# Delta sublayer: where a unit's corner and joining product stand among the next unit's doublings

## The reference, cut to what matters

```python
q, k, v = (silu(causal_conv4(x @ W)) for W in (Wq, Wk, Wv))      # conv over tokens, 4 taps
alpha, beta = sigmoid(x @ Wa + ba), sigmoid(x @ Wb + bb)
def step(S, (qt, kt, vt, at, bt)):                                # one token after another
    err = S @ kt - vt
    S = at * S - bt * err * kt.T
    return S, S @ qt
o = layernorm(scan(step)(q, k * DK**-0.5, v, alpha, beta))
out = (o * sigmoid(x @ Wg)) @ Wo
```

## Time and profile before

| what | value |
|---|---|
| median of 3 runs | 3333.66 us (3332.99 to 3333.68) |
| profiled execution, its own time | 3329.28 us |
| span in that execution | 3327.5 us |
| PE busy | 3193.5 us (96%) |
| PEld busy | 2639.1 us (79%) |
| DVE busy | 2411.1 us (72%) |
| ACT busy | 1955.1 us (59%) |
| POOL busy | 827.1 us (25%) |
| doubling products with d_power, L1652 | 4096 records, 142.2 us |
| taps on DVE, L1404 | 1116 records, 624.0 us |

### The profile page before, as it was taken

The page is one execution under the profiler, slowest core; times in us unless marked ns, Lnnn a source line. Parts: engine busy times, 40 slices in busy tenths (PEclk is TensorE's granted clock), DMA queues, the critical chain, the costliest instruction groups (busy, mean ns, idle before and its releaser), DMA issues. The chain is left out here.

```text
span 3327.5 us, 89349 instructions
## 1 busy us (share of the span) xinstructions
PE 3193.5 (96%) x34218; PEld 2639.1 (79%) x34218; DVE 2411.1 (72%) x7923; ACT 1955.1 (59%) x4769; POOL 827.1 (25%) x828
## 2 busy tenths in 40 slices
PE   6999989999999999999999969999799999999999
PEld 5888878888888888888888858788667777777787
DVE  4777778777778878787878637777666777777764
ACT  3565556666666666666666626565465555555553
POOL 2333322232222223232322223333200111111100
PEclk9999999999999999999999979999999999999999
DMA  6000000000000000000000040000000000000000
GB/s 242 1 1 1 1 8 27 22 21 18 15 18 25 18 25 18 22 16 21 21 22 21 9 163 1 1 1 1 1 1 1 1 1 1 1 5 5 5 8 10
DMA packets 51337, 66.84 MB, mean 20 GB/s; under 512 B 4962, under 2 KB 40290, under 8 KB 49378
## 3 DMA queue, kind: packets, MB, share of 16 engines
q1 hardware_dynamic: 50914, 61.13, 5.8%
HBM read 58.56 MB, written 2.56 MB: 18 GB/s over the span
## 5 line engine op out<-in xcount | busy, mean ns | idle before, releaser
L1404 DVE SCALAR_TENSOR_TENSOR d_acc<-d_raw,d_taps,d_acc 128x255 f32<-128x255 f32 x1116 | 624.0, 600 | 128.0 <-ACT d_raw L1392 114.8
L2485 ACT ACTIVATE s_probs<-s_probs,s_nmax 128x128 f32<-128x128 f32 (+1 forms) x768 | 286.8, 446 | 176.7 <-DVE s_nmax L203 176.0
L1659 ACT COPY d_power<-bank 128x768 f32<-128x768 f32 x320 | 259.5, 811 | 134.7 <-PE bank L1652 134.7
L203 DVE CUSTOM_DVE_ANT_0 s_probs<-bank,mask 128x128 f32<-128x128 f32 (+1 forms) x768 | 225.5, 349 | 105.7 <-PE bank L2466 105.6
L746 POOL TENSOR_TENSOR a_q<-a_rope 64x512 f32<-64x512 f32 x128 | 165.0, 1289 | 534.4 <-DVE a_recip L814 313.6
L1390 ACT ACTIVATE d_acc<-bank,d_tap_bias,d_taps 128x256 f32<-128x256 f32 x372 | 190.4, 563 | 148.0 <-PE bank L1368 138.2
L783 ACT ACTIVATE a_area<-a_area,a_nmax 128x128 f32<-128x128 f32 (+1 forms) x512 | 226.4, 443 | 85.6 <-DVE a_nmax L203 84.9
L203 DVE CUSTOM_DVE_ANT_0 a_area<-bank,mask 128x128 f32<-128x128 f32 (+1 forms) x512 | 159.0, 355 | 133.3 <-PE bank L764 130.9
L809 ACT COPY a_area<-bank 128x512 f32<-128x512 f32 (+1 forms) x260 | 137.3, 580 | 117.8 <-PE bank L800 117.8
L736 DVE TENSOR_TENSOR a_rope<-bank,a_sinT 32x512 f32<-32x512 f32 x256 | 177.4, 693 | 5.7
L1807 POOL TENSOR_TENSOR d_o_rs<-d_o_var,minus_half 128x4 f32<-128x4 f32 x64 | 69.6, 1088 | 419.7 <-DVE d_o_var L1801 419.7
(11 more groups left out here) (287 smaller groups left out, 8702.0 us busy)
## 6 DMA issues: line engine op xcount, KB each, us to landing
d_alpha<-d_alpha_rows SPq DMA_DIRECT2D x64, 256.0 KB, 3.6
d_g_decay<-d_running_rows SPq DMA_DIRECT2D x32, 258.0 KB, 3.5
a_w_o<-in_a_w_o SPq DMA_DIRECT2D x2, 2048.0 KB, 16.6
a_area<-in_a_q_nope SPq DMA_DIRECT2D x2, 1536.0 KB, 8.1
x<-in_x SPq DMA_DIRECT2D x8, 256.0 KB, 16.0
d_wk<-in_d_wk SPq DMA_DIRECT2D x1, 2048.0 KB
d_wq<-in_d_wq SPq DMA_DIRECT2D x1, 2048.0 KB
d_wv<-in_d_wv SPq DMA_DIRECT2D x1, 2048.0 KB
```

The costliest lines, as they stand in the source:

```text
L203: return core.nc.vector.tensor_tensor_reduce(out=out, in0=scores, in1=core.mask[:, blocks], scale=-1.0, scalar=HIGHEST, op0=ALU.add, op1=A ...
L1404: last = nc.vector.scalar_tensor_tensor(out=convolved(G, r)[:, j, d:T], in0=raw[:, r % 2, j, 0:T - d], scalar=taps[:, r // 2, h, 3 - d:4 - ...
L1659: nc.scalar.copy(power[:], b_step[:, :, 0:3 * P]).then_inc(g.step_out, 1)
L2485: last = nc.scalar.activation(own, own, ACT.Exp, scale=-1.0, bias=nmax[:, s % 2, t, i:i + 1])
```

## The change

Corner and join of unit e = u - 1 move from the end of round u - 1 into round u: corner ahead of doubling 0, join ahead of doubling 1 (behind kk and ab), and y from behind doubling 0 to behind doubling 1. A round then has six blocks of small tiles. Corner's product now goes to b_join (the banks of y and o) and no longer to the last columns of b_step, so the waits for those banks move from join to corner. Both get semaphores of their own (close_in_psum, close_out), and a unit has six steps on the old ones. ACT's queue gets the same order: corner's copy, doubling 0's copy, [ab], join's copy, doubling 1's copy, y's copy, then the sigmoids. Nothing is computed otherwise, and no DMA is moved.

```diff
--- before.py
+++ after.py
@@ -1150,7 +1150,7 @@
 UNITS = NB * CHUNKS
 ALL_GROUPS = NB * GROUPS
 LEVELS = 6
-STEPS = LEVELS + 2
+STEPS = LEVELS
 HALF = P // 2
 TAPS = 4
 RPG = 8
@@ -1181,6 +1181,7 @@
         self.k_in_psum, self.k_ready = sem("d_k_in_psum"), sem("d_k_ready")
         self.kq_decayed = sem("kq_decayed")
         self.step_in_psum, self.step_out = sem("d_step_in_psum"), sem("d_step_out")
+        self.close_in_psum, self.close_out = sem("d_close_in_psum"), sem("d_close_out")
         self.y_in_psum, self.y_ready = sem("dy_in_psum"), sem("dy_ready")
         self.yw_ready = sem("yw_ready")
         self.state_in_psum, self.state_ready = sem("state_in_psum"), sem("state_ready")
@@ -1495,7 +1496,7 @@
 
         def n_act(act, u):
             act.wait_ge(g.n_in_psum, u + 1)
-            need(act, g.step_in_psum, STEPS * (u - 2) + LEVELS + 1)
+            need(act, g.close_in_psum, 2 * (u - 2) + 1)
             nc.scalar.copy(wide(n0[u % 2][:]), b_kk[:, :]).then_inc(g.n_ready, 1)
 
         def k_pe(pe, u):
@@ -1599,7 +1600,7 @@
 
             if l == 0:
                 pe.wait_ge(g.n_ready, u + 1)
-            need(pe, g.step_out, STEPS * u + l if l > 0 else STEPS * u - 1)
+            need(pe, g.step_out, STEPS * u + l)
             lo_a = 2 * P
 
             def tile(s, r, lo, width):
@@ -1669,45 +1670,45 @@
         def corner_pe(pe, u):
 
             pe.wait_ge(g.step_out, STEPS * u + LEVELS)
-            for j in range(GH):
-                pair, c = j // 2, j % 2
-                cols = slice(3 * P + pair * HALF, 3 * P + (pair + 1) * HALF)
-                nc.tensor.matmul(b_step[half(c), 0, cols], tT[half(0), u % 2, j, half(0)],
-                                 core.ident[half(0), half(0)], start=True, stop=True,
-                                 tile_position=(0, c * HALF), skip_group_check=True)
-                last = nc.tensor.matmul(b_step[half(c), 1, cols], n0[u % 2][half(1), j, half(0)],
-                                        tT[half(1), u % 2, j, half(1)], start=True, stop=True,
-                                        tile_position=(HALF, c * HALF), skip_group_check=True)
-            last.then_inc(g.step_in_psum, 1)
-
-        def corner_act(act, u):
-            act.wait_ge(g.step_in_psum, STEPS * u + LEVELS + 1)
-            nc.scalar.copy(corner[:], b_step[:, :, 3 * P:4 * P]).then_inc(g.step_out, 1)
-
-        def join_pe(pe, u):
-
-            pe.wait_ge(g.step_out, STEPS * u + LEVELS + 1)
             need(pe, g.y_ready, u)
             need(pe, g.oT_affine, u)
             need(pe, g.rhs_ready, (u + 1) // 2 if u % 2 == 1 else 0)
             for j in range(GH):
                 pair, c = j // 2, j % 2
                 cols = half(pair)
+                nc.tensor.matmul(b_join[half(c), 0, cols], tT[half(0), u % 2, j, half(0)],
+                                 core.ident[half(0), half(0)], start=True, stop=True,
+                                 tile_position=(0, c * HALF), skip_group_check=True)
+                last = nc.tensor.matmul(b_join[half(c), 1, cols], n0[u % 2][half(1), j, half(0)],
+                                        tT[half(1), u % 2, j, half(1)], start=True, stop=True,
+                                        tile_position=(HALF, c * HALF), skip_group_check=True)
+            last.then_inc(g.close_in_psum, 1)
+
+        def corner_act(act, u):
+            act.wait_ge(g.close_in_psum, 2 * u + 1)
+            nc.scalar.copy(corner[:], b_join[:, :, 0:P]).then_inc(g.close_out, 1)
+
+        def join_pe(pe, u):
+
+            pe.wait_ge(g.close_out, 2 * u + 1)
+            for j in range(GH):
+                pair, c = j // 2, j % 2
+                cols = half(pair)
                 last = nc.tensor.matmul(b_join[half(0), c, cols], corner[half(c), 0, cols],
                                         corner[half(c), 1, cols], start=True, stop=True,
                                         tile_position=(c * HALF, 0), skip_group_check=True)
-            last.then_inc(g.step_in_psum, 1)
+            last.then_inc(g.close_in_psum, 1)
 
         def join_act(act, u):
-            act.wait_ge(g.step_in_psum, STEPS * (u + 1))
+            act.wait_ge(g.close_in_psum, 2 * (u + 1))
             heads = tT[half(0), u % 2, :, half(1)].rearrange("p (q s) t -> p s q t", s=2)
             nc.scalar.copy(heads, b_join[half(0), :, 0:P].rearrange("p s (q t) -> p s q t", q=2))\
-                .then_inc(g.step_out, 1)
+                .then_inc(g.close_out, 1)
 
 
         def y_pe(pe, e):
             c = e % 2
-            pe.wait_ge(g.step_out, STEPS * (e + 1))
+            pe.wait_ge(g.close_out, 2 * (e + 1))
             if c == 0:
                 pe.wait_ge(g.v_ready, e + 1)
             else:
@@ -1871,16 +1872,20 @@
                 for u in range(UNITS + 1):
                     e, n, q = u - 1, u % CHUNKS, rounds_of(u)
                     live = u < UNITS
+                    if e >= 0:
+                        corner_pe(pe, e)
                     if live:
                         step_pe(pe, u, 0)
-                    if e >= 0:
-                        y_pe(pe, e)
                     if u + 1 < UNITS:
                         kk_pe(pe, u + 1)
                     if n == CHUNKS - 2 and u + 2 < UNITS:
                         ab_pe(pe, u // CHUNKS + 1)
+                    if e >= 0:
+                        join_pe(pe, e)
                     if live:
                         step_pe(pe, u, 1)
+                    if e >= 0:
+                        y_pe(pe, e)
                     if q is not None:
                         project_pe(pe, q)
                     if live:
@@ -1910,15 +1915,12 @@
                         oT_pe(pe, e)
                     if live:
                         qk_pe(pe, u)
-                        corner_pe(pe, u)
                     if q is not None:
                         project_pe(pe, q + 3)
                     if e >= 0:
                         out_pe(pe, e)
                     if n == CHUNKS - 3 and u + 3 < UNITS:
                         xnT_pe(pe, u // CHUNKS + 1, q + 4)
-                    if live:
-                        join_pe(pe, u)
 
             @block.vector
             def _(dve):
@@ -1972,18 +1974,22 @@
                     e, n, G, q = u - 1, u % CHUNKS, u // 2, rounds_of(u)
                     live, odd = u < UNITS, u % 2
                     ahead = G + 1 if G + 1 < ALL_GROUPS and live else None
+                    if e >= 0:
+                        corner_act(act, e)
                     if live:
                         step_act(act, u, 0)
+                    if n == CHUNKS - 2 and u + 2 < UNITS:
+                        ab_act(act, u // CHUNKS + 1)
+                    if e >= 0:
+                        join_act(act, e)
+                    if live:
+                        step_act(act, u, 1)
                     if e >= 0:
                         y_act(act, e)
                     if odd and ahead is not None:
                         sigmoid_act(act, ahead, 2)
                     if not odd and u < UNITS:
                         sigmoid_act(act, G, 5)
-                    if n == CHUNKS - 2 and u + 2 < UNITS:
-                        ab_act(act, u // CHUNKS + 1)
-                    if live:
-                        step_act(act, u, 1)
                     if q is not None:
                         evacuate_act(act, q)
                     if live:
@@ -2009,16 +2015,12 @@
                         oT_act(act, e)
                     if ahead is not None:
                         sigmoid_act(act, ahead, 4 if odd else 1)
-                    if live:
-                        corner_act(act, u)
-                        if not odd:
-                            k_act(act, u)
+                    if live and not odd:
+                        k_act(act, u)
                     if q is not None:
                         evacuate_act(act, q + 3)
                     if n == CHUNKS - 3 and u + 3 < UNITS:
                         xnT_act(act, u // CHUNKS + 1, q + 4)
-                    if live:
-                        join_act(act, u)
 
             @block.gpsimd
             def _(pool):
```

## The result

The changed kernel takes 3354.29 us, the median of 4 runs (3348.10 to 3357.00), against 3333.67 (3332.99 to 3334.84) for the kernel before: a ratio of 1.0059, 95% interval 1.0041 to 1.0076. It is 20.6 us slower; 17.9 were forecast, in a range of 3338 to 3360. The profiled execution took 3357.00, with a span of 3355.2. One execution of the kernel before, in the comparison of e8, took 8075.17 us, a slow one; ratios and spreads here go by the fast runs alone.

What follows compares the result with a forecast made beforehand. TensorE's order was taken as the bound, with waits on POOL and DVE. Odd rounds to state 20.6, out - 9.6, even beginnings + 7.5, round 0 - 0.6: + 17.9 us, median 3351.6, range 3338 to 3360.

Steps and rivals of the forecast that it cites:

- out's restart of 0.10: On TensorE, a block following a wait costs 0.10 us more; charged to out, leaving an odd round 0.31 gained.
- Part 1: Corner's own block goes, 0.57 us less TensorE work per round; out's wait for POOL leaves 0.31 odd, 0 even.
- Rival A: The block on TensorE is saved in every round with no wait in its place: 20.4 us less, 3313; chance 0.06.
- Part 2: Corner merged with doubling 0 stays at 1.24 us; join ahead of doubling 1 adds 0.25 to every round's beginning.
- Part 3: y behind doubling 1, kk directly behind doubling 0: order sums to 0, but kk newly waits 0.56 to 0.89 in odd rounds.
- Rival B: kk finds its d_kT in time because DVE's even-round work slides forward: + 1.2 us, 3335, no change; chance 0.11.
- Rival C: Chain corner, copy, join, copy, y runs late behind doubling 1, adding 6 to 12 us: 3358 to 3364; chance 0.08.
- the 0.57 of round 37: Round 37's odd-round delay before state: kk's new wait for d_kT on TensorE, entered in its sum as 0.57 us.
- the 0.53: State's existing wait for DVE's d_yw in round 37, 0.53 us, which was to go as kk's new wait swallows it.

Runs made afterwards that it cites:

- e8: The kernel before with one edit, d_yw ahead of the third taps on DVE in odd rounds: 3326.24 us against 3333.36, ratio 0.9980.
- e3: The kernel before without its corner products and their copy, join reading a tile of zeros: 3322.88 us against 3333.76, ratio 0.9968.
- e5: The changed kernel with every join product done twice, same operands and place: 3368.26 us, 14.0 more than the changed kernel.
- e2: The changed kernel with DVE's second d_kT of an even round computed ahead of d_pT: 3338.71 us, 15.6 less than the changed kernel.
- e1: The kernel before with only kk moved ahead of y, directly behind doubling 0: 3345.53 us against 3333.76, ratio 1.0038.
- e6: The changed kernel with out moved to the next round behind doubling 0, and kk behind y: 3327.00 us against 3333.86 for the kernel before.
- e7: The changed kernel with out behind doubling 0, kk behind y, and d_yw ahead of the third taps on DVE: 3308.10 us against 3333.86 before.

## Why the prediction was right

Round lengths, from one start of out to the next (L1846 before, L1847 after), hold every term of the steady part. They are the same in every period to 0.02, but for rounds 2 and 17 after, and for round 61, which has the length of a round with remainder 1 or 3 in both kernels.

| rounds | before | after | difference | forecast |
|---|---|---|---|---|
| even, 0, 2, 4 | 21.65 | 22.01 | + 0.36 | 0.25 + 0.10 |
| even, 6 | 24.78 | 25.14 | + 0.36 | 0.25 + 0.10 |
| odd, 1 and 3 | 22.10 | 22.50 | + 0.40 | 0.82 - 0.41 |
| odd, 5 | 22.73 | 22.50 | - 0.23 | 0.19 - 0.41 |
| odd, 7 | 22.47 | 22.90 | + 0.43 | 0.84 - 0.41 |

The forecast put out's restart of 0.10 into the odd round's gain (0.41 - 0.10 = 0.31); between starts of out it falls into the even round.

**Part 1** was right in both halves: out is held by POOL at once in the even round, after 0.41 in the odd one. e3 shows it without anything else of the change. Rival A, the full saving, is out: it gave 3313 for the changed kernel and 3298 for e3, and 3354 and 3323 were measured.

**Part 2**: corner with doubling 0 takes 1.25 (1.24 was taken), join with doubling 1 takes 1.10 (1.10), and e5 gives 0.23 for a further join (0.25). The bounds from 0 to 0.35 were wider than needed.

**Part 3**: kk starts 0.56 later behind corner and doubling 0 in odd rounds with remainder 1, 3 and 5 than in even ones, and 0.95 later in those with remainder 7, against 0.57, 0.56 and 0.96 as worked out. Undone in the changed kernel (e2) or made in the kernel before (e1) it moves the time by 15.6 and 11.8, for 17 and 13 expected. Rival B, the level time without that wait (3335), is 4 under what e2 measures, and it needed an edit on DVE to come about. Rival C did not occur: y starts 0.2 after join's copy could release it.

**What was off** is at the ends. Round 1 was booked with no wait of kk, and it has one of 1.1, because in the kernel before y itself stood waiting there (0.60, for join's copy) and hid how late d_kT is. On balance it cost nothing: from qk in round 0 to the first out it is 24.62 before and 23.97 after, 0.65 less, and 0.66 less was booked (0.6 and 0.31, less 0.25). What stands ahead of that is 0.6 later, by this execution's clock: from 499.5 to 503 us the granted clock is 1.00 before and 0.50 after. Round 2 is 0.65 longer than its kind, by a pause inside doubling 1, and round 17 by 0.27, between join's start and y's; the pause in round 2 has the releaser "issue", and the cause of both stays open. In round 64 corner, copy, join and copy come in series: 1.40 longer, with 0.44 less in round 62, where 0 was booked. Together these are 2.5 us: the last out starts 20.4 later in the profiled execution, for 17.9 forecast. So the forecast was a little low, inside the range.

**Two of its signs did not come as written.** State was to wait in a quarter of the odd rounds with 0.3, which its own sum did not hold (the 0.57 of round 37 covers the 0.53); state waits for d_yw in no round. And the even round from its first projection to out was to be as long as before: round 32 takes 15.76 before and 15.63 after. That out comes earlier after its projection was named as a sign of being wrong; what it shows is that this projection spans 1.89 and no longer 1.99, so the chain that hangs on its end starts 0.10 sooner, and the chain itself is unchanged to 0.03.

One thing was passed over: d_yw was said to have y two blocks early. In round 31 after, the taps on DVE end at 1207.64 and y's copy at 1207.58; it was a draw. It cost nothing: state starts at 1210.47, 0.91 after d_yw's end.

## What to carry to other kernels

A wait that the profile shows as small, in nearly every round, marks two chains that arrive together; a saving ahead of it is worth only the other chain's slack, and here two timeline rows gave that to 0.01 us before anything was built (0.41, and 0.42 in e3). When an operation is moved forward in an in-order queue, look up when its last operand was ready, not whether it waited in its old place. And when a wait is lifted, ask which result of the same producer is needed next: here d_kT, then d_yw, both on one DVE run. With out's and kk's waits lifted the kernel gained 7 us (e6), with state's too it gained 26 (e7), of which 7 come without the merged blocks (e8).

## What the runs showed of the hardware

d_yw on DVE, four instructions, spans 0.87 in the earlier trace rows; in the changed kernel it spans 1.94, with a POOL product beside it:

```profile
1207.62 1.94 DVE L1738 TENSOR_SCALAR d_yw<-d_y,d_last_w 128x128 f32<-128x128 f32 x4
1208.19 1.28 POOL L1433 TENSOR_TENSOR d_qT<-d_acc,d_sigm 128x512 f32<-128x512 f32 x1 [8.77 <-ACT d_sigm L1415]
...
1208.21 1.34 DVE L1738 TENSOR_SCALAR d_yw<-d_y,d_last_w 128x128 f32<-128x128 f32 x1
```

The last row is the fourth of the four by itself: it started 0.02 after POOL's product and took 1.34, where the median of a d_yw is 0.28. DVE ended at 1209.56, POOL at 1209.47. Before, the same POOL product (at 1195.56 in round 31) ran beside the taps, and the taps of round 31 after take 2.69 where they took 3.72: the delay of about 1.0 went from one to the other. The Trainium skill (SBUF — State Buffer, Who interferes with whom) says of the port pair that DVE and GpSimd share that the one that issues first has it for the whole instruction, and the other is blocked; these rows agree.
